# A gated cross-attention block on one core: consecutive rows in a pair of tiles, a seventh warm-up product, scores by bank, another order of GpSimd's early work and of the last products

## What is computed

```python
def flamingo(x, ctx, g_xattn, g_ffn, Wq, Wk, Wv, Wo, bo, w1, b1, w2, b2):
    # x (2, 1024, 256), ctx (2, 77, 256); 8 heads of 64; hidden layer of 1024
    q, k, v = layernorm(x) @ Wq, ctx @ Wk, ctx @ Wv            # split into 8 heads
    attn = softmax(q @ k.T / 8) @ v                            # over the 77 context rows
    x = x + tanh(g_xattn) * (attn @ Wo + bo)
    h = relu(quant(quant(layernorm(x)) @ quant(w1).T + quant(b1)))   # 8 bits, fixed point
    return x + tanh(g_ffn) * (quant(h) @ quant(w2).T + quant(b2))
```

## Time and profile before

| | |
|---|---|
| time, median of 3 runs | 120.07 us (119.46 to 120.09) |
| the profiled execution | 120.01 us |
| its span, first to last instruction | 118.2 us |
| TensorE busy | 111.8 us (95%) |
| VectorE busy | 97.7 us (83%) |
| GpSimd busy | 89.1 us (75%) |
| ScalarE busy | 76.4 us (65%) |
| chain that ended last | TensorE 52%, GpSimd 21%, VectorE 14%, DMA 5% |
| granted TensorE clock, mean | 0.998 |

### The profile page before, as it was taken

The page is one execution under the profiler, slowest core; times in us unless marked ns, Lnnn a source line. Parts: engine busy times, 40 slices in busy tenths (PEclk is TensorE's granted clock), DMA queues, the critical chain, the costliest instruction groups (busy, mean ns, idle before and its releaser), DMA issues.

```text
span 118.2 us, 2898 instructions
## 1 busy us (share of the span) xinstructions
PE 111.8 (95%) x1012; PEld 102.1 (86%) x1012; DVE 97.7 (83%) x223; ACT 76.4 (65%) x169; POOL 89.1 (75%) x161
## 2 busy tenths in 40 slices
PE   7979997899999999999999999999999999999990
PEld 2659976899798999988999999999999999897870
DVE  3029798999999999989999999999797979648981
ACT  4137766869688894998667575748483819448420
POOL 4003587698796989898989978996899999988720
PEclk9999999999999999999999999999999999999999
DMA  4989799300000000000010002000200020020204
GB/s 80 315 247 386 280 375 399 152 0 8 0 3 0 6 3 0 0 6 0 0 74 15 6 0 89 0 3 6 89 0 0 3 89 6 0 89 8 88 13 165
DMA packets 5328, 8.87 MB, mean 75 GB/s; under 512 B 1191, under 2 KB 2242, under 8 KB 5186
## 3 DMA queue, kind: packets, MB, share of 16 engines
q1 hardware_dynamic: 5082, 8.34, 20.1%
q10 hardware_dynamic: 232, 0.34, 0.9%
HBM read 6.59 MB, written 2.10 MB: 73 GB/s over the span
## 4 chain that ended last, share of the span: by engine, by line
PE 52%; POOL 21%; DVE 14%; DMA 5%; issue 3%; ACT 1%; SPq 1%; POOLq 0%; DVEq 0%; ACTq 0%
PE sc_ps L841 15%; PE of_ps L878 12%; PE h_ps L910 7%; DMA wq_sb<-in_L_xattn_Wq_dram 5%; POOL hid L362 5%; POOL x_sb L383 4%; PE of_ps L925 4%; POOL probs L300 4%; POOL rstd L310 3%; POOL yq L316 3%; DVE probs L614 3%; PE tr_ps L853 3%; DVE mx L609 3%; DVE den L621 2%; DVE pT L650 1%
## 5 line engine op out<-in xcount | busy, mean ns | idle before, releaser
L841 PE MATMUL sc_ps<-a_sb,xT 128*128 128x308 f32 x192 | 31.1, 311 | 0.7 <-DVE probs L614 0.7
L878 PE MATMUL of_ps<-u_sb,pT 128*128 128x256 f32 x240 | 30.9, 281 | 0.1
L878 PEld LDWEIGHTS of_ps<-u_sb,pT 128*128 128x128 f32 x240 | 29.5, 188 | 0.3 <-issue 0.3
L841 PEld LDWEIGHTS sc_ps<-a_sb,xT 128*128 128x128 f32 x192 | 27.4, 188 | 1.4 <-issue 1.2
L438 ACT ACTIVATE probs<-probs,rstd 128x616 f32<-128x616 f32 x16 | 13.1, 818 | 23.0 <-DVE probs L614 23.0
L481 ACT ACTIVATE hid_q<-h_ps,b1z 128x256 int8<-128x256 f32 x58 | 24.5, 494 | 3.6 <-PE h_ps L910 3.6
L300 POOL TENSOR_TENSOR probs<-probs,rden 128x616 f32<-128x616 f32 x16 | 19.5, 1221 | 1.9 <-DVE rden L624 1.9
L362 POOL CAST hid<-hid_q 128x512 bf16<-128x512 int8 x27 | 15.8, 611 | 2.0 <-ACT hid_q L481 2.0
L910 PE MATMUL h_ps<-x2T,w1T 128*128 128x256 bf16 x128 | 16.7, 274 | 0.0
L609 DVE TENSOR_REDUCE mx<-sc_ps 128x8 f32<-128x616 f32 x16 | 12.6, 787 | 2.8 <-PE sc_ps L841 2.7
L614 DVE TENSOR_TENSOR probs<-sc_ps,mx 128x616 f32<-128x616 f32 x16 | 12.8, 800 | 0.5
(11 more groups left out here) (124 smaller groups left out, 175.8 us busy)
## 6 DMA issues: line engine op xcount, KB each, us to landing
w_sb<-in_L_ffn_w_dram SPq DMA_DIRECT2D x2, 1024.0 KB, 10.9
out_dram<-x_sb SPq DMA_DIRECT2D x7, 256.0 KB, 2.5
x_sb<-in_x_dram SPq DMA_DIRECT2D x4, 256.0 KB, 8.0
x_sb<-in_x_dram SPq DMA_DIRECT2D x1, 1024.0 KB, 9.8
wq_sb<-in_L_xattn_Wq_dram SPq DMA_DIRECT2D x1, 512.0 KB, 5.8
wv_sb<-in_L_xattn_Wv_dram SPq DMA_DIRECT2D x1, 512.0 KB, 7.8
wo_sb<-in_L_xattn_Wo_dram SPq DMA_DIRECT2D x1, 512.0 KB, 8.6
wk_sb<-in_L_xattn_Wk_dram SPq DMA_DIRECT2D x1, 256.0 KB, 3.4
```

What stands on the lines that cost most here:

```text
L841: ins = nc.tensor.matmul(sc_ps[:, a, 0:HALF], xT[:, T % 2, p, c, :], a_sb[:, q, T // TB, c, HALF * a:HALF * a + HALF], start=first, stop=last)
L878: ins = nc.tensor.matmul(attn_ps, pT[:, T % 2, p, P * c:P * c + P], u_sb[:, q, MC * (T // TB) + c, :], start=first, stop=last)
```

## The change

1. A pair of tiles holds consecutive rows: tile pair j is rows 256j to 256j + 255 of a batch entry, partition p has rows 256j + 2p and 256j + 2p + 1. A pair's DMA then covers 256 KB of memory without a hole, and the load of the second batch entry has four pieces of 2 KB per partition in place of one of 8 KB.
2. Seven warm-up products in place of six; the 256-column one behind the transposes of ctx is gone.
3. `scores` does all six products of bank 0 and then those of bank 1, with a count of `scores_ready`, `max_ready` and `centered` for each bank. For tiles 0 and 1 `center` works bank by bank, for the others on both at once.
4. VectorE's, ScalarE's and GpSimd's starts are put in another order; slot 0 of the loops is partly moved ahead of the loop.
5. GpSimd scales first in slots 1 and 2 (`softmax_scale(s + 1)` ahead of `normalise_second(s - 1)`), rstd_first(2, 4) follows softmax_scale(0), and output_bias moves from slot 1 to slot 3.
6. attend(0) takes the low part of pT ahead of the low part of u.
7. At the end tile 14's last four products stand ahead of the last six of tile 15.

The diff, cut to its core:

```diff
-WARM = 6
+WARM = 7
+LOW_FIRST = ((0, 0), (1, 0), (0, 1))
-    x_v = x.rearrange("b (p t) d -> p b t d", p=P)
-    out_v = out.rearrange("b (p t) d -> p b t d", p=P)
+    x_v = x.rearrange("b (j p t) d -> p b j t d", p=P, t=2)
+    out_v = out.rearrange("b (j p t) d -> p b j t d", p=P, t=2)
...
 # GpSimd
             a1_parts(0)
-            rstd_first(2, 4)
             bias_parts()
             softmax_scale(0)
+            u_low(0, 1)
             bias_rows(0)
-            u_low(0, 1)
+            rstd_first(2, 4)
             hidden_bias()
             for s in range(TILES):
+                if s in (1, 2):
+                    softmax_scale(s + 1)
                 if live(s - 1):
                     normalise_second(s - 1)
-                if live(s + 2):
+                if live(s + 2) and s not in (1, 2):
                     softmax_scale(s + 1)
...
-                if s == 1:
+                if s == 3:
                     output_bias()
                 if s in (2, 3):
                     u_low(1, s - 2)
...
 # ScalarE
             minus_centred(2)
-            minus_centred(3)
             act.wait_ge(v_psum, 2)
             nc.scalar.copy(values_of(1), values_psum(1)).then_inc(v23_ready, 1)
+            exponentials(0)
             xT_copy(2)
-            exponentials(0)
+            minus_centred(3)
...
             for s in range(TILES):
+                if s == 0:
+                    pT_copy(0)
+                    xT_copy(3)
                 if live(s + 1):
                     exponentials(s + 1)
-                pT_copy(s)
-                if live(s + 3):
+                if s > 0:
+                    pT_copy(s)
+                if s > 0 and live(s + 3):
                     xT_copy(s + 3)
...
 # VectorE
-            stats_first(2, 4)
-            center(0)
+            stats_first(2, 3)
+            center(0, (0,))
+            center(0, (1,))
+            stats_first(3, 5)
+            denominators(0)
             rowsT_low(2)
-            stats_first(4, 5)
-            denominators(0)
             u_low(0, 0)
-            center(1)
+            center(1, (0,))
+            center(1, (1,))
+            probsT_low(0)
+            denominators(1)
             u_low(0, 2)
-            stats_first(5, 6)
+            rowsT_low(3)
...
                 if live(s + 2):
                     center(s + 2)
+                if s == 0:
+                    stats_first(5, 6)
...
 # TensorE, scores
-                for p, q in PARTS:
...
-                    for c in range(DK):
-                        for a in range(2):
+                for a in range(2):
+                    if T >= 1:
+                        pe.wait_ge(centered, 2 * T - 1 + a)
+                    for p, q in PARTS:
...
+                        for c in range(DK):
...
-                ins.then_inc(scores_ready, 1)
+                    ins.then_inc(scores_ready, 1)
...
 # TensorE, the end
-            for half in range(2):
-                for T in (TILES - 2, TILES - 1):
-                    ffn_half(T, half)
+            ffn_half(TILES - 2, 0)
+            ffn_chunks(TILES - 1, 0, 2)
+            ffn_half(TILES - 2, 1)
+            ffn_chunks(TILES - 1, 2, FC, last=True)
```

More of the change, by code:

```diff
@@ L598, in stats_first @@
             def stats_first(first, end):
-                dve.wait_ge(x_in[min(first, TB) // 2], 16)
                 for T in range(first, end):
+                    dve.wait_ge(x_in[min(T, TB) // 2], 16)
                     nc.vector.bn_stats(st1[:, T, :], x_sb[:, T, :]).then_inc(st1_done, 1)
@@ L604, in stats_first, with maxima, subtract_maxima, center @@
                     nc.vector.bn_aggr(mv1[:, T, :], st1[:, T, :]).then_inc(mv1_ready, 1)
[L606 to L611, removed]
+            def maxima(T, banks):
+                i, h = T % 2, slice(H // 2 * banks[0], H // 2 * banks[-1] + H // 2)
+                dve.wait_ge(scores_ready, 2 * T + banks[-1] + 1)
+                nc.vector.tensor_reduce(mx[:, i, h].rearrange("p (a h) -> p a h", a=len(banks)),
+                                        sc_v[:, banks[0]:banks[-1] + 1, :, :], AX.X, ALU.max).then_inc(max_ready, len(banks))
+            def subtract_maxima(T, banks):
+                i, h = T % 2, slice(H // 2 * banks[0], H // 2 * banks[-1] + H // 2)
+                dve.wait_ge(max_ready, 2 * T + banks[-1] + 1)
                 if T >= 2:
                     dve.wait_ge(pT_psum, T - 1)
-                nc.vector.tensor_tensor(probs_v(T).rearrange("p (a h) m -> p a h m", a=2), sc_v,
-                                        mx[:, i, :].rearrange("p (a h) -> p a h", a=2).unsqueeze(3)
-                                        .to_broadcast([P, 2, H // 2, M]), ALU.subtract).then_inc(centered, 1)
+                nc.vector.tensor_tensor(probs_v(T)[:, h, :].rearrange("p (a h) m -> p a h m", a=len(banks)),
+                                        sc_v[:, banks[0]:banks[-1] + 1, :, :],
+                                        mx[:, i, h].rearrange("p (a h) -> p a h", a=len(banks)).unsqueeze(3)
+                                        .to_broadcast([P, len(banks), H // 2, M]), ALU.subtract).then_inc(centered, len(banks))
+            def center(T, banks=(0, 1)):
+                maxima(T, banks)
+                subtract_maxima(T, banks)
             def denominators(T):
@@ L724, in _ @@
                     stats_second(s - 1)
[L725 to L729, removed]
+                if s > 0:
+                    if live(s + 1):
+                        denominators(s + 1)
+                    probsT_low(s)
+                    if live(s + 3):
+                        rowsT_low(s + 3)
                 if s == 4:
@@ L869, in attend @@
                     pe.wait_ge(bo_rows, 2)
-                for p, q in PARTS:
+                parts = PARTS if T > 0 else LOW_FIRST
+                for p, q in parts:
                     if p == 1:
@@ L876, in attend @@
                     for c in range(MC):
-                        first, last = (c, p, q) == (0, *PARTS[0]), (c, p, q) == (MC - 1, *PARTS[-1])
+                        first, last = (c, p, q) == (0, *parts[0]), (c, p, q) == (MC - 1, *parts[-1])
                         ins = nc.tensor.matmul(attn_ps, pT[:, T % 2, p, P * c:P * c + P], u_sb[:, q, MC * (T // TB) + c, :],
@@ L887, in quantisedT @@
                 else:
[L888 removed]
+                    pe.wait_ge(centered, 2 * TILES)
                     if T - 2 in yT_last:
@@ L923, in ffn_half, with ffn_chunks @@
                     pe.wait_ge(hid_ready, K_LAST + k)
-                for c in range(4 * half, 4 * half + 4):
+                ffn_chunks(T, 4 * half, 4 * half + 4, last=half == 1)
+            def ffn_chunks(T, first, end, last=False):
+                p, i = T // 2, T % 2
+                for c in range(first, end):
                     ins = nc.tensor.matmul(ffn_of(T), hid[:, p, c, i, :], w2T[:, c, :], start=(c == 0), stop=(c == FC - 1))
-                if half == 1:
+                if last:
                     ins.then_inc(ffn_psum, 1)
```

29 lines of the change are left out of this document (13 added, 16 removed).

## The result

The changed kernel is slower: 120.88 us against 119.86 us (medians of 22 runs each, taken in turn on the same chips), a ratio of 1.0096 with a 95% interval of 1.0078 to 1.0114, so +0.9 to +1.4 us. 120.9 us and 0.9 us more than before were forecast. The profiled execution took 120.66 us with a span of 118.8 us, against 120.01 and 118.2.

A forecast was written before the change was run, and what follows sets the result against it. VectorE was taken to pace 25.44 to some 52 us, then TensorE, then both TensorE and GpSimd nearly full. 120.01 us plus net 0.9 for GpSimd's debt (the start's 0.1 included) gave 120.9 us, range 119.4 to 121.4.

The forecast's parts named there:

- The bounds by stretch: Wait for wq, then dependent start to 25.4 us, VectorE to some 52, TensorE to 80.4, then chain through GpSimd.
- The debt on GpSimd: Gapless GpSimd work from rden(3), including output_bias, delays probsT(5) by 1.2 us; 0.3 returns at attend(6), net +0.9 us.
- Scaling first brings nothing: Slots 1 and 2: probsT(2) comes some 0.8 us earlier, without gain because quantisedT and attend still wait for VectorE.
- The start: Tiles 0 and 1 on VectorE: residual(0) at 25.34 instead of 25.44 us, 0.1 us gained; bounds -0.7 to +0.9.
- The walk: Event-by-event timing of VectorE's reordered start, from bank 0 at 13.9 us to residual(0) at 25.34 us.
- both new gaps: VectorE idles 0.4 us each before denominators(0), behind exponentials(0), and before probsT_low(0), behind copies of pT and xT.
- The split: Centring tiles 0 and 1 by bank costs VectorE 0.5 us; two halves take 0.14 us more than one whole.
- The layout: New row order of x in loads and stores: 0, bounds ±0.2 us; only the last store could change.
- Warm-up: Seventh product added, 256-column product removed: 0 with cover from the 0.85 us wait for wq, +0.45 us without.
- The sign: For the warm-up: TensorE's wait for wq falls to some 0.4 us.
- The end: Last products: tile 14's sum 0.2 us earlier, but the last store hangs on tile 15; 0, bounds ±0.1 us.
- Tile 15's sum comes when it came: Reordering the last products leaves tile 15's sum, on which the last store hangs, at its old time: 0.

The follow-up runs named there:

- a_unsplit: Changed kernel with tiles 0 and 1 centred in one operation each: 121.81 us, ratio 1.0142 to the kernel before.
- b_warm: Kernel before with seven warm-up products and without the 256-column one: 119.83 us, ratio 1.0008 to the kernel before.
- b_layout: Kernel before with only the new order of rows in loads and stores: 119.76 us, repeated 119.10 us, ratio 0.9960 both times.
- c_start_only: Changed kernel with GpSimd's loop and last products as before and counts raised by one: 119.61 us, ratio 0.9975 to the kernel before.
- a_loop_order: Changed kernel with GpSimd's loop as before (output_bias in slot 1, no scaling first): 119.69 us, ratio 1.0000 to the kernel before.
- a_bias_slot1: Changed kernel with output_bias back in slot 1, scaling first kept: 119.83 us, ratio 1.0002 to the kernel before.
- b_vector_extra: Kernel before with an unused 256-element fill on VectorE in each of slots 1, 2 and 3: 120.99 us, ratio 1.0114.

## Why the prediction was right, point by point

- *The bounds by stretch*: right. In the changed kernel VectorE is gapless in slots 1 to 4, at one distance from residual to residual up to residual(3); in slot 5 it waits 0.44 us for scores that the debt holds up. The added fills show the bound for slots 1 to 3 by experiment.
- *The debt on GpSimd*, the term that carries the sum: right in place and mechanism, and in size partly by luck. Forecast: softmax_scale(5) ends at 46.45, probsT(5) starts at 46.5, 1.2 us later, 0.3 us comes back at attend(6), net 0.9. Profile after: 46.49, 46.55, 1.27, and 0.30 back (attend(6) at 55.99, 0.97 after 55.02). Alone in the kernel before it costs 0.80 us anchored and a ratio of 1.0061; put back in the changed kernel it returns the ratio to 1.0002. But the profile after reached the anchor 0.38 us sooner than that of before, by its loads and key products. Counted from the anchor softmax_scale(5) was forecast to end at 33.80 us (46.45 - 12.65) and ended at 34.22 (46.49 - 12.27), and attend(6) came 1.35 us later, not 0.9. Of the 0.42 us missing, 0.30 were there when softmax_scale(3) started (20.25 where 19.95 was forecast): the start and the raises by two. The other 0.12 is in GpSimd's row, 13.97 us long where the sum had 13.85.
- *Scaling first brings nothing*: right, twice. probsT(2) is 0.45 us earlier from the anchor (28.86 - 12.27 = 16.59, against 29.69 - 12.65 = 17.04; 0.8 was forecast), and quantisedT(1) waits 0.59 us for residual(2) where it had waited 0.20.
- *The start*: wrong in sign, small in size. Forecast 0.1 us gained, measured 0.17 us lost at residual(0). The walk had every event and both new gaps. What it mis-sized were the times in between: bank 0 was centred 0.1 us later than I put it, and by the second gap's end (probsT_low(0), 8.52 us from the anchor where I had 8.35) it was 0.17 us. The last 0.10 came behind that. Most of that last part could not be read in the rows of before: a subtraction that waits for a count raised by two starts 0.07 us later. That also lengthens each slot of VectorE by 0.06 us, which the sum had at nothing.
- *The split*: its price was right (halves of 0.48 us); its worth was underrated, by half, when a_unsplit was forecast. The reading that attend's products and those of the scores differ by under 1% per column was wrong (15 of 256 columns in 1.76 us, 12 of 308 in 1.77: some 4%), but the 0 drawn from it held: from scores to attend it is 1.78 us before (36.36 to 38.14) and after (36.27 to 38.05).
- *The layout*: the step that put it at 0 failed, and its bounds of 0.2 us were a little tight. The rows of before couldn't show the new pitch: the last store lands 0.3 us sooner, in every profile with the new rows, and the kernel is 0.24 us faster anchored in both of its profiles. The Trainium skill (DMA: Bandwidth & Descriptors, Anatomy of one DMA) puts most of the fixed cost on the receipt, in a section on DMAs issued by GpSimd, where these are SyncE's; no run here splits it off, but what it says can't be read as "the order of rows doesn't matter".
- *Warm-up*: 0, right. The sign failed: the wait for wq did not fall to 0.4 us but was gone both in the profile after, where TensorE waited 0.71 us for wk ahead of the keys (the prediction had wq as the only load that anything waits for), and in b_warm. The rule that activity releases the clock (the Trainium skill, TensorE: Matmul & The Clock Gate, "What's actually happening") gave the keys nothing here that shows: in the one profile with only the warm-up changed they ran slower, and slow and fast keys stand in profiles with six products and with seven.
- *The end*: forecast 0 within 0.1, measured +0.07 anchored and 0.09 by the rows: right. The step "Tile 15's sum comes when it came" is off by that much.

Together, going from version to version in anchored time: -0.24 for the order of rows (b_layout), +0.06 for start and warm-up (c_start_only), +0.48 for the raises by two and the last products (a_loop_order), -0.10 for scaling first (a_bias_slot1), +0.78 for output_bias in slot 3 (the changed kernel). Such a chain must add up to the 0.98 us between the two profiles; a single step is good to some 0.1 us. Taken off alone from the changed kernel the raises were worth 0.07, since the debt hides them, so the terms depend on their surroundings.

The total of the forecast, +0.9 us, is just below the interval of the ratio (+0.9 to +1.4 us). Its closeness has luck in it: start and raises cost 0.3 us or more beyond what the sum had, the layout gained 0.24 where it had 0, and the 120.9 us met the median of 120.88 from a base of 120.01 us where the median of before is 119.86.

None of the versions is clearly faster than before. The best is the kernel before with the new order of rows, 0.996 in both series, each interval reaching to 1.000.

## What to carry to other kernels

Before moving work on an engine to another slot, add up that engine's operations from the last gap ahead of the new place to the next operation that somebody waits for: work that leaves a stretch with idle time and enters one without is paid in full at that operation, however early the engine was elsewhere. Alone in the kernel before, the 1.07 us of output_bias moved probsT(5) by 1.22 us and the end by 0.80. Serving an engine earlier than it can use the result brings nothing while another engine paces the slots; adding a small known operation to the suspected pace-maker settles which one does. And when profiles of single executions are compared, count from an event behind the loads and ahead of the change, since the landing of a load and the pace of the first products can differ more than the effect looked for. A profile that hits the forecast in microseconds of the span can then turn out to hide two misses. And a small cost that vanishes when it is taken off alone may only lie in the shadow of a larger one: take the larger one off first.

## What the runs showed of the hardware that was not expected

- A semaphore raised by two instead of one by a VectorE operation lets the next VectorE operation that waits for it start 0.07 us later: 0.87 us against 0.80 from start to start, and over all tiles centred whole 0.86 to 0.91 in the four versions with the raise by two, 0.79 to 0.84 in the ten others; raised by one again, it was 0.80 again.
- Storing 256 KB to consecutive memory landed in 2.0 us, to pieces of 2 KB 8 KB apart in 2.5 us; 128 KB in pieces of 1 KB, 2 KB apart, in 1.7 us, 8 KB apart in 2.0 us.
- The load of wq, 512 KB, third in SyncE's queue, took 4.7 to 6.5 us from issue to landing from one execution to the next. Where it was late TensorE waited for it, up to 1.51 us (b_layout), and everything behind moved along.
- The first twelve key products took 1.8 to 3.5 us from one execution to the next at a granted clock that reads 1.00, and the loads of weights among them 0.19 to 0.34 us. In b_vector_extra wq landed soonest of all (4.7 us), and the anchor was still at 13.99 us: the products held it up, not the load.
